# Starting the transfers of the maxima's rows from ScalarE instead of SyncE, in a planned one-core transformer kernel

## The reference, cut to what matters

```python
for l in range(LAYERS):                                   # 6 layers
    keys = jnp.concatenate([past, x], axis=1)
    q = (x @ Wq.T + bq).reshape(B, T, HEADS, HEAD_DIM)    # 16 heads of 8
    k = (keys @ Wk.T + bk).reshape(B, T + H, HEADS, HEAD_DIM)
    v = (keys @ Wv.T + bv).reshape(B, T + H, HEADS, HEAD_DIM)
    scores = jnp.einsum('bqhd,bkhd->bhqk', q, k) / jnp.sqrt(jnp.asarray(HEAD_DIM, x.dtype))
    scores = jnp.where(valid[None, None], scores, neg)    # delta from 0 to 125
    attn = jax.nn.softmax(scores, axis=-1)
    o = jnp.einsum('bhqk,bkhd->bqhd', attn, v).reshape(B, T, C)
    x = _ln(x + o @ Wo[l].T + bo[l], ln1_g[l], ln1_b[l])
    ff = jax.nn.gelu(x @ W1[l].T + b1[l], approximate=False) @ W2[l].T + b2[l]
    x = _ln(x + ff, ln2_g[l], ln2_b[l])
```

## Time and profile before

| | |
|---|---|
| time, median of 3 runs | 1104.46 us (1101.13 to 1105.72) |
| profiled execution | 1104.54 us |
| its span, first to last instruction | 1102.7 us |
| PE busy | 994.2 us (90%) |
| DVE busy | 809.7 us (73%) |
| ACT busy | 763.1 us (69%) |
| POOL busy | 407.5 us (37%) |
| mean granted TensorE clock | 0.972 |

### The profile page before, as it was taken

The page is one execution under the profiler, slowest core; times in us unless marked ns, Lnnn a source line. Parts: engine busy times, 40 slices in busy tenths (PEclk is TensorE's granted clock), DMA queues, the critical chain, the costliest instruction groups (busy, mean ns, idle before and its releaser), DMA issues.

```text
span 1102.7 us, 47422 instructions
## 1 busy us (share of the span) xinstructions
PE 994.2 (90%) x20080; PEld 705.4 (64%) x20080; DVE 809.7 (73%) x2451; ACT 763.1 (69%) x1418; POOL 407.5 (37%) x544
## 2 busy tenths in 40 slices
PE   1679999999999999999998999998987988899993
PEld 0356777777777777777775777666664544555772
DVE  6777887777778887777777775879798979872320
ACT  7457666767777667767773777767767868688741
POOL 8711433333344433333344213444646353401311
PEclk9769999999999999999998999999999989999997
DMA  5522211222225211332224123221112020401220
GB/s 160 116 62 61 61 42 42 78 70 61 62 62 105 56 43 41 64 89 62 61 62 103 27 38 61 60 46 29 35 28 60 3 61 4 117 26 37 68 77 10
DMA packets 72627, 64.80 MB, mean 59 GB/s; under 512 B 16226, under 2 KB 66914, under 8 KB 72418
## 3 DMA queue, kind: packets, MB, share of 16 engines
q1 hardware_dynamic: 72418, 61.78, 23.3%
HBM read 15.70 MB, written 1.05 MB: 15 GB/s over the span
## 4 chain that ended last, share of the span: by engine, by line
PE 72%; DVE 11%; ACT 5%; POOL 5%; issue 3%; SPq 1%; DMA 1%; POOLq 0%; DVEq 0%; ACTq 0%
PE b L775 11%; PE b L887 9%; PE b L878 8%; PE b L676 7%; PE b L756 5%; PE b L790 4%; PE b L959 4%; PE b L949 4%; PE b L709 4%; PE b L806 2%; PE b L846 2%; PE b L871 2%; DVE mx L1218 2%; ACT probs L1021 2%; PE b L862 2%
## 5 line engine op out<-in xcount | busy, mean ns | idle before, releaser
L1021 ACT ACTIVATE probs<-b 128x443 f32<-128x443 f32 (+2 forms) x736 | 354.0, 543 | 137.5 <-PE b L756 96.5
L1218 DVE TENSOR_REDUCE mx<-b 128x2 f32<-128x378 f32 (+1 forms) x768 | 353.0, 508 | 93.9 <-PE b L709 93.5
L676 PE MATMUL b<-band,identb 64*64 64x252 bf16 x2304 | 170.4, 286 | 18.4 <-DVE mx L1218 8.1
L775 PE MATMUL b<-probs,vals 128*32 128x189 f32 (+5 forms) x3968 | 182.8, 311 | 1.2 <-DVE mx L1218 0.3
L775 PEld LDWEIGHTS b<-probs,vals 128*32 128x32 f32 x3968 | 115.1, 110 | 47.2 <-issue 12.2
L1543 POOL TENSOR_SCALAR veps<-mv 128x4 f32<-128x4 f32 x48 | 11.0, 230 | 352.4 <-DVE mv L1324 352.4
L756 PE MATMUL b<-qpack,kpack 64*64 64x189 bf16 (+5 forms) x3968 | 137.0, 236 | 0.3 <-issue 0.3
L709 PE MATMUL b<-kpack,qpack 62*64 62x189 bf16 (+1 forms) x3072 | 122.0, 239 | 1.0 <-issue 1.0
L676 PEld LDWEIGHTS b<-band,identb 64*64 64x64 bf16 x2304 | 67.0, 105 | 83.6 <-issue 36.5
L887 PE MATMUL b<-w,hid 128*128 128x128 f32 x768 | 110.1, 287 | 0.0
L1215 DVE TENSOR_REDUCE mx<-b 128x1 f32<-128x512 f32 (+7 forms) x256 | 99.3, 444 | 14.1 <-PE b L724 13.7
(11 more groups left out here) (173 smaller groups left out, 1695.7 us busy)
## 6 DMA issues: line engine op xcount, KB each, us to landing
kpack<-kparts SPq DMA_DIRECT2D x168, 128.2 KB
qpack<-qparts SPq DMA_DIRECT2D x168, 128.0 KB, 3.4
qpack<-mrows SPq DMA_DIRECT2D x224, 4.0 KB
w<-in_w SPq DMA_DIRECT2D x12, 256.0 KB, 4.3
w<-in_wa SPq DMA_DIRECT2D x12, 256.0 KB, 3.3
w<-in_wb SPq DMA_DIRECT2D x12, 256.0 KB, 3.7
rowt<-in_rowt SPq DMA_DIRECT2D x6, 384.0 KB, 3.4
stream<-in_x SPq DMA_DIRECT2D x4, 256.0 KB, 4.0
```

The lines of the kernel that those rows point to most:

```text
L676: pe.matmul(out, identb[rows, rows], rhs.unsqueeze(1).to_broadcast([64, 2, 2, EDGE]), start=True, stop=False, skip_group_check=True)
L775: mm = pe.matmul(bank("sum", u, group)[32 * j:32 * j + 32, q0:q0 + w - skip], vals[:, u % 2, at:at + 32], probs[:, n % SETS, j, col + skip ...
L1021: act.activation(probs[:, n % SETS, j, 0:width], bank("exp", u, v, b)[:, 0:width], ACT.Exp, scale=SCALE).then_inc(a_emptied, 1)
L1218: red = dve.tensor_reduce(out[:, 2 * tb:2 * tb + 2], read[:, 0:2 * width].rearrange("p (t k) -> p t k", k=width), AX.X, ALU.max)
```

## The change

`maxrows` becomes a job of ScalarE. The function `load_max` moves from the SyncE program to the ScalarE program: wait until the copy into `mrows` is done (`a_emptied`), then start the 4 transfers, now on ScalarE's own DMA queue. The numbers in the plan change too: cost 1720 in place of 2150, landing 2300 in place of 2500. Transfers, sizes, semaphores and what waits for them are the same.

```diff
-            add("sp", ("maxrows", u, half), 2150, [("mrows", u, half)], line="maxrows", landing=2500)
+            add("act", ("maxrows", u, half), 1720, [("mrows", u, half)], line="maxrows", landing=2300)
...
         @block.scalar
         def _(act):
+            def load_max(u, half):
+                act.wait_ge(a_emptied, emptied("parts", u, half))
+                for part in range(PARTS):
+                    for h in range(2):
+                        first = 1 + (2 * h + half) * 2 * SEQ
+                        act.dma_start(qpack[BODY + part:P:64, u % BUFS, first:first + 2 * SEQ],
+                                     mrows[:, part * P + 64 * h:part * P + 64 * h + 64]).then_inc(max_loaded, 16)
...
                 elif kind == "mrows":
                     copy_parts(*where)
+                elif kind == "maxrows":
+                    load_max(*where)
```

More of the change, by code:

```diff
@@ L1700, in pack @@
                     sp.dma_start(dest, parts_[:, n, :]).then_inc(packed, 16)
[L1702 to L1708, removed]
             def load_expert(b, r):
@@ L1747, in _ @@
                     pack(u, which)
-                elif kind == "maxrows":
-                    load_max(*where)
                 elif kind == "expert":
```

## The result

The changed kernel takes 1220.29 us (median, 1216.96 to 1222.93) beside 1104.49 us for the kernel before: ratio 1.105, 95% interval 1.1016 to 1.1089. It is slower, as predicted, but by 116 us and not by 56, and the time lies outside the range of 1122 to 1190.

The account below looks back on a forecast made before the run. PE was taken as the bound in the middle, any wait lengthening the kernel. Eleven units at 3.1 us made 34; with 5, 5, 7 and 2 that is 53, plus 3 for the clock on 1104.5: 1160 us, range 1122 to 1190.

Parts of the forecast that it names:

- the change gains nothing directly: PE's DMA waits: 2.3 us in all, none for the maxima's rows, so a faster start of these gains near 0.
- The burst, forecast at 2.11 us: On ScalarE: four starts take 2.11 us a burst, as on SyncE, with bounds of 0 and 3.4 us.
- The period of 34 us: Middle, about 250 to 550 us: the time from one unit to the next goes from 30.9 to about 34 us.
- The norm chain of 6.74 us: From `out` to the first `norm`: the layer norm's chain takes 6.74 us; PE has 4.12 of work, so waits 2.6.
- mending one of the two waits would leave the other: Between `out` and `norm`: the 2.2 us burst wait and 2.6 us norm wait are parallel; mending either leaves the other.
- waits forecast for the page: PE's waits list: `weigh` (L775) on ACT's `probs` and `norm` on DVE's `ztok`, some 2 to 3 us each.
- in parallel, covered and not added: Same PE stretch before `norm`: the 2.2 us behind the burst are covered by the layer norm's 2.6, not added.
- I take one fall, 3: PE's clock in the twelve units: one fall to 1.2 GHz, costing 3 us, with bounds of 0 to 36.
- the clock falls in most of the twelve units: Rival for units 5 to 16: falls add 36 us to the 53, giving 1190 to 1200 us; chance 0.12.
- The units at the edge: Units outside the repeating part: 2 and 3 wait 2.3 us each; 0, 4, 17, 18 and 19 about 1 each.
- a tenth of the bursts and 2 us of shape changes on the path: Outside units 5 to 16: a tenth of 68 us of bursts, 7 us (bounds 0 and 30), plus 2 for shape changes.
- stages after 600 us by more than 15 us: Sign of being wrong: the middle is as said, but stages before 120 or after 600 us move over 15 us.

Follow-up runs that it names:

- e6: Kernel before with its old job order, only the burst of each unit's second half started by ScalarE, the first half's by SyncE: 1128.3 us.
- e11: Changed kernel's job order, but SyncE makes the starts, and in units 6 to 17 starts the k pack before the maxima's rows: 1194.5 us.
- e12: Kernel with the new order, SyncE starts and k pack first, plus one more POOL power in the first layer norm of units 5 to 16: 1219.1 us.
- e3: Changed kernel with the first half's burst one job later on ScalarE, behind the `exp` that PE needs: 1208.6 us.
- e1: Kernel before with its whole old job order, only the transfer starts moved to ScalarE, right behind their copies: 1201.7 us.
- e7: Old job order with ScalarE starts, but two starts of four per burst, the second bf16 part's rows left out: 1131.6 us.

## Why the prediction was wrong in size

**Right.** That the change gains nothing directly: no run with the rows started by ScalarE is faster in either stretch than the kernel before, e6's middle (0.8 us) apart, which is within the spread. The burst, forecast at 2.11 us: it takes 2.2 to 2.9 in the middle. The period of 34 us: 34.3 and 34.0 in the two periods whose clock holds, though eight of the ten with the short distance lost their clock. The norm chain of 6.74 us: 6.66 in e11, and e12 shows that it is the bound of the new order. That mending one of the two waits would leave the other: e3 and e11 take away the burst's and the norm's remains, e1 has only the burst's. Of the waits forecast for the page, that for `probs` came, at L676 and not at L775; that for `ztok` did not (0.5 us in the middle), since the burst's wait hides it.

**The step "in parallel, covered and not added".** It was off by 0.7 us a unit. I looked for the reader of the data that the late `exp` makes and found `weigh`. PE was stopped one job earlier, by the bank that this `exp` empties, so 1.3 us of work came behind the wait. The error nearly cancelled against another one. I summed PE's work between `out` and `norm` to 4.12 us, so 2.6 of wait; e11 shows 6.66 - 1.23 - 0.61 = 4.82 of work and 1.84 of wait. Together 3.1 was predicted, and 3.0 stands in the rows: the size was hit by luck, the places of the waits were not.

**The step "I take one fall, 3".** This is the largest miss in the middle. The eight periods with a fall among those of units 7 to 14 took 288.6 us, against 8 x 34.2 with the clock held: 15 us. The two in the periods of units 4 and 5 took 34.3 and 34.1 us, where e11, whose clock holds there, has 32.5 and 32.1: 4 us more, 1.4 of it the burst's by the 0.7 us above. So the ten falls cost some 17 to 19 us in the middle, an estimate, where 3 stood for the whole kernel. In the late part 29 us more are at 1.2 GHz, worth 14 at most, and PE's busy time grew by 13.6 there. I had reasoned from unit 16 alone and took the new gap, about 2 us of work in 5.4, to be shallower and so safer. The gap that came is as deep as unit 16's: 0.89 us of work in 3.70, beside 0.76 in 3.00. The bounds, 0 to 36, hold what the clock took; the value in them was chosen badly. The rival "the clock falls in most of the twelve units" is what happened in the middle, ten falls, though a fall cost a little under 2 us and not 3.

**The units at the edge.** For units 0 to 4 together 6.6 us were set (1, 0, 2.3, 2.3 and 1). The five periods that hold their waits came out 6.3, 3.8, 3.4, 1.6 and 3.8 us longer, 18.9 in all; less 2 to 4 for two falls, 8 to 10 us are missing. With the clock's 14 to 16 that accounts for the miss in the middle, 24 us: the prediction's terms put there 6.6, ten units at 3.1 and one fall, some 41; 65.5 were measured.

**The step that put a tenth of the bursts and 2 us of shape changes on the path outside the repeating part.** With units 15 and 17 to 19 the prediction's terms make some 12 us for the late part; it measured 49. This is the largest miss of all. The step asked what the bursts do there. On the new order they do nothing. The order does it, 47.5 us in e11 without any start on ScalarE. I had treated a new plan as the old one with a few displaced jobs, and costed only those. The prediction named this as what would make it wrong (stages after 600 us by more than 15 us), but gave the new order there no term and no width, and the range ended at 1190 because of it.

What is open: which displaced jobs make the late part long; and why one gap makes the clock fall and its twin does not.

## What to carry to other kernels

A DMA start holds an in-order compute engine for half a microsecond, so ask which instruction stands behind it and who needs its result or its buffer; the same burst cost 45.6 us in one place and nothing in another. When an edit makes a planner run again, cost the new order as a second change, with a range of its own from the plan's unevenness, and freeze the order to test either alone. On an engine with no slack, a wait of a microsecond or two may also cost clock: 10.4 us of added waits cost 24.9 here.

## What the runs showed of the hardware

- A start on ScalarE's queue takes 0.518 us at the median (0.508 to 1.142) for 4 KB, on SyncE's 0.495. What stands behind a burst begins only when its last start is made: 562.40 + 2.52, then `exp` at 564.98. What stands ahead of it can still run: in e3 a table load of 1.28 us begins at 806.27 and three starts at 806.28.
- Losses of this kind don't add: 98 and 90 us apart give 116 together. In the middle both waits stand in the same stretch of PE, between `out` and `norm`.
- After a gap with 0.89 us of work in 3.70 the granted clock fell to 0.50, after one with 0.89 in 3.60 it stayed at 1.00. With waits shorter by 1.28 us than in e1 (e7) it didn't fall in the middle at all. The Trainium skill's page "TensorE: Matmul & The Clock Gate" (section "HAM oscillation — how this bites in real kernels") describes a kernel that waits in each round and starts each next round slow. The trace agrees in kind, ten falls in 15 periods, but here the clock didn't fall in every round.
